# Four-stage transformer block: first tile's rows of the experts fetched in the second attention; its first batch loaded and normalised beside the end of the first attention

## The chip, the cores and the metric

The program runs on one core of a Trainium2 chip. The metric is the device time of one execution in microseconds; of several executions the median is taken. Engines are named as in the profile: PE is TensorE's matmul, PEld its weight load, DVE is VectorE, ACT is ScalarE, POOL is GpSimd, SP is SyncE, which here only issues DMAs.

## What is computed

Input x is 8 batches of 512 tokens of 256 numbers, in float32. Two layers follow each other:

```
xn = layernorm(x)
x  = x + attention0(xn) + ffn0(xn)
xn = layernorm(x)
x  = x + attention1(xn) + experts(xn)

attention0: latents of 128, 16 heads of 64, rotary positions, full softmax
ffn0:       256 -> 1024 -> 256 with binarised weights, gelu
attention1: 16 heads of 16, q = elu(q) + 1, k = elu(k) + 1, causal sums
            out = q . cumsum(k v) / max(q . cumsum(k), 1e-6)
experts:    gate = softmax(xn @ Wg + bg), the best 2 of 8 experts chosen
            for e in 8: out += chosen[e] * (relu(xn @ W1[e] + b1[e]) @ W2[e] + b2[e])
```

The result of a matmul must hold float32 accuracy: each factor is split into a high part and a rest ("hi" and "lo"), and three matmuls (L103 to L105) make one product.

## The kernel before

The program is four stages, one after the other: stage_f (ffn0 and the latents), stage_a (attention0), stage_b (attention1 and the choice of the experts), stage_c (the experts). Each stage is a block with a program for each engine; a block ends when every engine is through, and its last DMAs are among that. Only then does the next block begin. The order within an engine is written out by hand; engines wait for each other on semaphores.

**End of stage_a.** DVE inverts the last denominators (`invert`, L1065), ACT takes over the last values (L1147), PE projects, DVE adds (L1122), and SP stores the last batch in mid_x and waits for it.

**Stage_b** works batch by batch, in slots t = 0 to 3. Its head, L1390 to L1421 on SP, fetches batch 0 of x, the identity, the raw weights q, k and v, ten small tables (`later`), batch 1, and 2 MB of the first expert's weights. DVE then runs `norm_variance(0)`, `norm(0)`, the low halves of the weights (L1731), waits for all ten tables, makes batch 0 in four slots `make(0, t)`, and then does `norm_variance(1)`, `norm(1)`, before the loop over batches. `make(b, 3)` on DVE holds `weigh_experts` and `choose`. ACT runs `norm_root(0)`, the high halves of the weights (L1845), `make(0, t)`, `norm_root(1)`. PE transposes the normalised batch (L1448), projects (L103 to L105), and goes into the loop: scores (L1487), then the transposes of batch 1. POOL writes each token's row to the lists of its two experts by indirect DMA (L1924); ACT pads the end of every list with one tile of rows that point to a spare token (L1839).

**Stage_c** runs eight experts e. Expert e has as many tiles of 256 tokens as its list needs (`tiles_of`, a value loaded from `trips`). In this run they are 7, 5, 3, 7, 1, 1 for e = 0 to 5 and 12 for the last two together. SP loads a tile's rows (L2048) into the one buffer c_x_t, PE transposes them (L2068), ACT and DVE make hi and lo, PE makes eight `up` and eight `down` products (m = 0 to 7), ACT and DVE turn each `up` into h_hi and h_lo (L2128, L2154), DVE adds the bias to y (L2168), POOL adds y's rows to the output (L2198) by token numbers that it has fetched (`load_ids`, L2187). There is one buffer y: DVE may write it only when `y_free` is given, which POOL does in `settle` (L2206) once the rows of the tile before have landed. In the kernel before, `settle` stands at the head of POOL's loop over tiles, and a first one is let through by a counted semaphore.

The weights of expert e + 2 are split while expert e (1 to 5) runs: in tile i, ACT casts piece k = 0 to 3 at m = 0, 2, 4, 6 (`cast`, L2114) and DVE subtracts (`split_low`, L2147). Tile 0 does the first half of the weights, tile 1 the second, and so in turn. POOL does the last piece always, and all four of the second half where the expert has one tile (`late`, L2234), **after** the tiles of e and before the next `settle`. One piece is a cast (L2177) and a subtraction (L2182). For e = 0 POOL splits all of w1 before its loop, and w2 in chunks within the loop with at least one chunk after it (`rest`, L2227).

```
                    if by_engines(e):
                        pool.wait_ge(tile_splits, e)
                        with pool.Fori(pool.value_load(late[0:1, e:e + 1], ...
```

## Time and profile before

| what | value |
|---|---|
| runs | 2082.5, 2083.79, 2087.86 us; median 2083.79 |
| the profiled execution | 2079.97 us, of which the span is 2078.3 us |
| PE busy | 1882.9 us, 91% of the span |
| DVE, ACT, POOL busy | 60%, 45%, 61% |
| mean granted TensorE clock | 0.964 of full |
| stage_f and stage_a | up to 1243.56 us |
| stage_b | 1243.56 to about 1599.7 us |
| stage_c | 1599.7 us to the end |

The profile is one execution. PE's busy share is high in every stage, so what counts is where PE stands idle and what ends that idle time: a timeline row shows it in square brackets. The granted clock is 1.00 when TensorE runs at 2.4 GHz and 0.50 at 1.2 GHz.

### The profile page before, as it was taken

How to read it: one execution, taken by the hardware profiler on the slowest of the kernel's cores; microseconds unless marked ns; L12 is line 12 of the kernel's file. 1: busy time of each engine (PE TensorE's matmuls, PEld its weight loads, DVE VectorE, ACT ScalarE, POOL GpSimd, SP SyncE). 2: the span in 40 equal slices, each digit the busy share in tenths (PEclk: the TensorE clock that was granted, in tenths of full speed). 3: DMA queues.
4: the chain of work that ended last, by engine and by line, in shares of the span. 5: the costliest groups of instructions: out<-in, count | busy, mean ns of one | idle time of the engine just before them, and what ended most of it. 6: DMA issues, size and time to landing. Idle time of an engine off the chain costs nothing. (4 is left out here: it accounts for less than half of the span.)

```text
span 2078.3 us, 35394 instructions
## 1 busy us (share of the span) xinstructions
PE 1882.9 (91%) x12820; PEld 1311.8 (63%) x12820; DVE 1244.4 (60%) x1819; ACT 931.8 (45%) x1605; POOL 1270.1 (61%) x824
## 2 busy tenths in 40 slices
PE   6997799999999999999999976888883899998998
PEld 5887444544545454454544545676762899998998
DVE  5775466656565666656666525776763566656343
ACT  5885344334343433434334224433320456776554
POOL 3553588778687887868778643455463664435433
PEclk8999799999999999999999988999996899999999
DMA  4223322232231323213232202132224443332222
GB/s 138 102 107 113 107 58 64 50 96 62 72 82 31 92 62 84 62 38 92 52 102 52 62 32 105 41 96 68 72 67 148 133 86 81 85 77 53 37 47 42
DMA packets 82432, 158.35 MB, mean 76 GB/s; under 512 B 14680, under 2 KB 64088, under 8 KB 76496
## 3 DMA queue, kind: packets, MB, share of 16 engines
q1 hardware_dynamic: 64832, 130.50, 22.6%
q0 software_dynamic: 14592, 18.40, 5.6%
q10 hardware_dynamic: 2880, 7.73, 1.0%
q8 instruction: 82, 1.34, 0.3%
q14 instruction: 46, 0.38, 0.1%
HBM read 80.45 MB, written 44.15 MB: 60 GB/s over the span
## 5 line engine op out<-in xcount | busy, mean ns | idle before, releaser
L1162 ACT ACTIVATE a_pr<-a_pT 128x1024 f32<-128x1024 f32 x256 | 261.8, 1023 | 425.3 <-PE a_pT L940 425.3
L1195 POOL TENSOR_TENSOR a_total<-a_total,a_pr 128x1024 f32<-128x1024 f32 x128 | 320.6, 2505 | 148.9 <-ACT a_pr L1162 148.5
L1051 DVE TENSOR_REDUCE a_row_max<-a_pG 128x2 f32<-128x1024 f32 x256 | 309.1, 1220 | 144.6 <-PE a_pG L914 144.3
L953 PE MATMUL a_pA<-a_pr,a_v 128*64 128x512 f32 x1024 | 277.4, 620 | 0.1
L2154 DVE TENSOR_TENSOR c_h_lo<-c_h,c_h_hi 128x256 fp32r<-128x256 f32 x288 | 151.3, 532 | 181.3 <-ACT c_h_hi L2128 181.0
L2128 ACT ACTIVATE c_h<-c_pU,c_b_c 128x256 f32<-128x256 f32 x288 | 140.8, 489 | 177.9 <-PE c_pU L105 176.6
L1195 POOL TENSOR_TENSOR a_total<-a_pr 128x1024 f32<-128x1024 f32 x64 | 151.7, 2370 | 51.4 <-ACT a_pr L1162 51.1
L1176 POOL TENSOR_TENSOR a_by_cos<-a_by_cos,a_swapped 128x1024 f32<-128x1024 f32 x64 | 155.4, 2429 | 36.7 <-DMA a_swapped<-a_by_sin 36.6
L1183 POOL TENSOR_TENSOR a_qk_lo<-a_by_cos,a_qk_hi 128x1024 fp32r<-128x1024 f32 x64 | 158.7, 2480 | 2.3 <-ACT a_qk_hi L1130 2.3
L1045 DVE TENSOR_TENSOR a_by_sin<-a_pG,a_sin 128x1024 f32<-128x1024 f32 x64 | 78.3, 1224 | 129.4 <-PE a_pG L105 124.7
L2198 POOL DMA_INDIRECT out_x<-c_y,c_ids x72 | 118.0, 1639 | 40.8 <-DVE c_y L2168 24.1
L2128 ACT ACTIVATE c_h_hi<-c_pU,c_b_c 128x256 fp32r<-128x256 f32 x288 | 139.9, 486 | 0.0
L914 PEld LDWEIGHTS a_pG<-a_qk_hi 64*128 64x128 f32 x512 | 45.9, 186 | 143.7 <-issue 91.0
L914 PE MATMUL a_pG<-a_qk_hi 64*128 64x512 f32 x512 | 120.8, 489 | 5.1 <-ACT a_qk_hi L1130 3.8
L1130 ACT CAST a_qk_hi<-a_by_cos 128x1024 fp32r<-128x1024 f32 x64 | 67.0, 1046 | 110.3 <-POOL a_by_cos L1176 110.3
L103 PE MATMUL c_pU<-c_xT_hi,d_w_lo 128*128 128x256 f32 x368 | 108.8, 296 | 7.3 <-remote 6.2
L935 PE MATMUL a_pT<-a_qk_hi,a_qk_lo 64*128 64x512 f32 x512 | 113.2, 436 | 1.9 <-ACT a_pr L1162 1.7
L103 PE MATMUL c_pY<-d_w_hi,c_h_lo 128*128 128x256 f32 x368 | 105.5, 287 | 8.5 <-DVE c_h_lo L2154 8.3
L940 PE MATMUL a_pT<-a_neg_max,a_ones 64*128 64x512 f32 x512 | 108.9, 419 | 0.0
L104 PE MATMUL c_pU<-c_xT_lo,d_w_hi 128*128 128x256 f32 x368 | 106.7, 290 | 0.0
L105 PE MATMUL c_pU<-c_xT_hi,d_w_hi 128*128 128x256 f32 x368 | 105.9, 288 | 0.0
L953 PEld LDWEIGHTS a_pA<-a_pr,a_v 128*64 128x64 f32 x1024 | 50.8, 135 | 86.9 <-issue 85.9
(271 smaller groups left out, 4986.3 us busy)
## 6 DMA issues: line engine op xcount, KB each, us to landing
a_swapped<-a_by_sin SPq DMA_DIRECT2D x256, 128.0 KB, 2.3
a_inv_by_head<-mid_inverses SPq DMA_DIRECT2D x30, 512.0 KB, 5.8
c_x_t<-mid_rows SPq DMA_DIRECT2D x37, 272.0 KB, 2.9
mid_latents<-f_c_parts SPq DMA_DIRECT2D x8, 1024.0 KB, 3.9
a_latent_parts<-mid_latents SPq DMA_DIRECT2D x8, 1024.0 KB, 7.4
d_raw<-in_weights SPq DMA_DIRECT2D x3, 2048.0 KB, 8.2
c_raw<-in_weights SPq DMA_DIRECT2D x3, 2048.0 KB, 7.7
f_x_t<-in_x SPq DMA_DIRECT2D x8, 512.0 KB, 3.8
```

The lines of the kernel that those rows point to most:

```text
L103: nc.tensor.matmul(out, l_lo, r_hi, start=start, stop=False, **kw)
L914: last = nc.tensor.matmul(pair[:, h, :], qk_hi[rows, u % RQ, 0, t * P:(t + 1) * P], qk_hi[rows, u % RQ, 1, :], start=True, stop=True)
L935: nc.tensor.matmul(pT[:, h, :], k[rows, 1, ks], q[rows, 0, :], start=(i == 0), stop=False)
L953: last = nc.tensor.matmul(pA[64 * h:64 * h + 64, :], v[:, t, p, h, :], pr[:, n % RP, h, :], start=(t == 0), stop=(t == NT - 1))
L1051: nc.vector.reduce_max(row_max[:, u % 2, :, t], pair[:], AX.X).then_inc(read, 1)
L1162: nc.scalar.activation(pr[:, n % RP, :, :], pT[:], ACT.Exp, scale=SCALE).then_inc(exp_done, 1)
L1176: nc.gpsimd.tensor_tensor(by_cos[:, u % 2, :, :], by_cos[:, u % 2, :, :], swapped[:], ALU.add).then_inc(rope_done, 1)
L1183: nc.gpsimd.tensor_tensor(qk_lo[:, u % RQ, :, :], by_cos[:, u % 2, :, :], qk_hi[:, u % RQ, :, :], ALU.subtract).then_inc(qk_lo_done, 1)
L1195: nc.gpsimd.tensor_tensor(total[:, u % 2, :, :], before, pr[:, n % RP, :, :], ALU.add).then_inc(summed, 1)
L2128: nc.scalar.activation(dst[:, m % RH, :], pU[m % RH][:], ACT.Relu, bias=b1_c[:, e, m:m + 1]).then_inc(relu_done[m % RH], 1)
L2154: nc.vector.tensor_tensor(h_lo[:, m % RH, :], h[:, m % RH, :], h_hi[:, m % RH, :], ALU.subtract).then_inc(h_lo_done[m % RH], 1)
L2198: pool.indirect_dma_start(out=out, out_offset=bass.IndirectOffsetOnAxis(ap=ids[:, t:t + 1], axis=0), in_=y[:, t, :], in_offset=None, compu ...
```

## The change

Names with `ahead` are tensors that now live over stages a, b and c: the identity, batch 0 of x, its normalised form xm (whose first half later takes the first expert tile), and raw q. The change does the following.

- In stage_a, SP loads batch 0 of x and raw q in the middle of the stage; DVE takes the variances before its last `invert`, ACT the root after its last copy, DVE normalises after `invert`.
- In stage_b the head is shorter: SP begins with raw k and v, then batch 1, then the tables. DVE goes `make(0, 0)`, `norm_variance(1)`, `make(0, 1)`, `norm(1)`, `make(0, 2)`, the wait for the tables, `weigh_experts(0)`; `choose(0)` comes after the first mask in the loop.
- At the end of stage_b, SP fetches the rows of the first expert's first tile; the first list gets two tiles of padding, and its number of tiles is at least two.
- Stage_c begins with the transposes of that tile. ACT, not SP, loads b1 and the weights of expert 3; SP begins with the second tile.
- POOL's `settle` stands at the end of each tile, and the first `y_free` comes from DVE.
- POOL's late pieces for expert e + 2 come **before** the tiles of e. ACT's cast of piece k = 3 waits for them.

```diff
@@ stage_a, SP
                     if u == 2 * NP:
                         sp.dma_start(tokens(x1, B), tokens(x1, 0)).then_inc(spare_done, 16)
+                        for dst, src in ((ahead.x, tokens(x1, 0)), (ahead.raw_q, l1_wq)):
+                            sp.dma_start(dst[:], src).then_inc(ahead_in, 16)
@@ stage_a, DVE
+                ahead_variance()
                 for half in range(2):
                     invert(UNITS // GROUP - 1, half)
+                ahead_norm()
@@ stage_a, ACT
                 take_values(UNITS - 1)
+                act.wait_ge(ahead_step, 2 * NT + 1)
+                nc.scalar.activation(small[:, 1, :], small[:, 0, :], ACT.Sqrt).then_inc(ahead_root, 1)
@@ stage_b, SP
-                load(0)
-                sp.dma_start(ident[:], ident_d).then_inc(ident_in, 16)
-                for i, (n, (src, _)) in enumerate(names.items()):
-                    sp.dma_start(raw[n][:], src).then_inc(raw_in[i], 16)
+                for n in "kv":
+                    sp.dma_start(raw[n][:], names[n][0]).then_inc(raw_in[n], 16)
+                load(1)
...
                         if b == B:
                             store(b - 2)
+                            first_rows()
@@ stage_b, DVE
-                dve.wait_ge(loaded, 16 * LATER)
-                for t in range(NT):
-                    make(0, t)
-                norm_variance(1)
-                norm(1)
+                make(0, 0)
+                norm_variance(1)
+                make(0, 1)
+                norm(1)
+                make(0, 2)
+                dve.wait_ge(loaded, 16 * LATER)
+                weigh_experts(0)
...
+                        if b == 0 and t == 0:
+                            choose(0)
@@ stage_c, ACT
+                    if k == PIECES // 2 - 1:
+                        act.wait_ge(late_done, e - 2)
                     nc.scalar.copy(w_hi[w][:, at], raw[w][:, at]).then_inc(cast_done[k], 1)
...
-                x_high()
+                act.dma_start(b1_c[:], b1).then_inc(b1_in, 16)
+                x_high(False)
                 load_weights(nc.scalar, 1)
                 act.dma_start(b2_row[:], b2).then_inc(b2_in, 16)
                 load_weights(nc.scalar, 2)
+                load_weights(nc.scalar, 3)
@@ stage_c, DVE
                 x_low()
+                dve.sem_inc(y_free, 1)
@@ stage_c, POOL
                 for e in range(NE):
+                    if by_engines(e):
+                        wait_raw(pool, e + 2)
+                        with pool.Fori(pool.value_load(late[0:1, e:e + 1], ...), PIECES // 2) as i:
+                            split_high(e + 2, i * PIECE + WIDE // 2, PIECE)
+                            split_low(e + 2, i * PIECE + WIDE // 2, PIECE)
+                        pool.sem_inc(late_done, 1)
                     with pool.Fori(0, tiles_of(pool, e)) as i:
-                        settle()
                         load_ids(row_of(e, i))
...
                         send()
...
+                        settle()
-                    if by_engines(e):
-                        pool.wait_ge(tile_splits, e)
...
-                        pool.sem_inc(splits, 1)
-                settle()
```

In `cast(e + 2, ...)` the number waited for is `(e + 2) - 2`, so in expert e ACT waits until POOL has done the pieces of this same e. The wait stands in every tile of the expert; from the second tile on it is met already.

The first place where order matters is DVE at the head of stage_b, before:

```order
L1731 TENSOR_TENSOR b_wv_lo<-b_raw_v,b_wv_hi 128x528
L1617 TENSOR_TENSOR b_xT_lo<-b_pG,b_xT_hi 128x512 x2
L1624 SCALAR_TENSOR_TENSOR b_qT<-b_pG,b_ex 128x512 x2
L1624 SCALAR_TENSOR_TENSOR b_kT<-b_pG,b_ex 128x512 x2
L1677 TENSOR_TENSOR b_lg<-b_lg,b_bg_row 128x32
...
L1702 TENSOR_SCALAR b_sel<-b_rank 128x32
L1592 BN_STATS b_stats<-b_x_t 128x6 x4
...
L1611 TENSOR_SCALAR b_xm<-b_x_t,b_small 128x256 x4
L1632 TENSOR_TENSOR d_scores<-b_pA,b_causal 128x2048
```

and now:

```order
L1773 TENSOR_TENSOR b_wv_lo<-b_raw_v,b_wv_hi 128x528
L1659 TENSOR_TENSOR b_xT_lo<-b_pG,b_xT_hi 128x512 x2
L1634 BN_STATS b_stats<-b_x_t 128x6 x4
...
L1666 SCALAR_TENSOR_TENSOR b_qT<-b_pG,b_ex 128x512 x2
L1647 RECIPROCAL b_small<-b_small 128x4
...
L1653 TENSOR_SCALAR b_xm<-b_x_t,b_small 128x256 x4
L1666 SCALAR_TENSOR_TENSOR b_kT<-b_pG,b_ex 128x512 x2
L1719 TENSOR_TENSOR b_lg<-b_lg,b_bg_row 128x32
...
L1674 TENSOR_TENSOR d_scores<-b_pA,b_causal 128x2048
L1688 TENSOR_TENSOR b_state<-b_pS,b_blocks 128x512
...
L1744 TENSOR_SCALAR b_sel<-b_rank 128x32
```

The statistics and xm of batch 1 have moved from behind the choice (b_sel) to between the features q and k of batch 0, and the choice itself behind the first mask and state.

The second place is POOL in stage_c between two experts. The rows between the sends of one expert's last tile and the next expert's first sends, before (c_ids_f is the fetch of the token numbers, `f_ones_set` the old name of the semaphore number that `settle` waits on, y_sent):

```order
L2198 DMA out_x<-c_y,c_ids 4352x256
L2234 TENSOR_LOAD d_late [waits f_base_done]
...
L2177 COPY d_w_hi<-d_raw 128x512
...
L2182 TENSOR_TENSOR d_w_lo<-d_raw,d_w_hi 128x512
...
L2014 TENSOR_LOAD d_trips
...
L2206 ISA [waits f_ones_set]
...
L2187 DMA c_ids_f<-mid_rows 128x2x1
L2193 CAST c_ids<-c_ids_f 128x2 [waits f_sign2_done,f_b2_in]
```

and now (there `settle` waits on the number once called f_w2s_in):

```order
L2256 DMA out_x<-c_y,c_ids 4352x256
L2264 ISA [waits f_w2s_in]
...
L2277 TENSOR_LOAD d_late [waits f_y_done]
...
L2235 COPY c_w_hi<-c_raw 128x512
...
L2240 TENSOR_TENSOR c_w_lo<-c_raw,c_w_hi 128x512
...
L2066 TENSOR_LOAD d_trips
...
L2245 DMA c_ids_f<-mid_rows 128x2x1
L2251 CAST c_ids<-c_ids_f 128x2 [waits f_ones_set,f_ln_in]
```

The settle has moved ahead of the pieces, and the pieces now belong to the expert whose tiles follow.

The third place is ACT in the first tile of an expert, at m = 5 to 7, now:

```order
L2185 ACTIVATE c_h<-c_pU,c_b_c 128x256
L2185 ACTIVATE c_h_hi<-c_pU,c_b_c 128x256
L2169 ISA [waits f_g_lo_done]
L2169 COPY d_w_hi<-d_raw 128x512
L2076 ISA [waits f_c_bias_done]
L2185 ACTIVATE c_h<-c_pU,c_b_c 128x256
L2185 ACTIVATE c_h_hi<-c_pU,c_b_c 128x256
L2160 CAST c_xT_hi<-c_pX 128x256 [waits f_diag_done] x2
```

The row with f_g_lo_done is the new wait (late_done has that number); before, this cast had none. Behind it on ACT stand the two activations of m = 7 and the casts of the next tile's rows.

## Rows read from the trace of the kernel before

**Rows 1.** Timeline, end of stage_a, DVE (start us, length us, instruction, [idle before <-releaser])

```profile
1222.34 3.37 DVE L1065 RECIPROCAL a_inv<-a_pD 128x256 f32<-128x256 f32 x2 [10.87 <-PE a_pD L962]
...
1230.39 1.45 DVE L1119 TENSOR_TENSOR a_att<-a_att,a_pT 128x512 f32<-128x512 f32 x2 [4.68 <-PE a_pT L997]
```

**Rows 2.** Timeline, head of stage_b up to the first projection

```profile
1247.44 1.41 DVE L1592 BATCH_NORM_STATS2 b_stats<-b_x_t 128x6 f32<-128x256 f32 x4 [7.24 <-DMA b_x_t<-mid_x]
...
1250.65 0.63 ACT L1845 CAST b_wv_hi<-b_raw_v 128x528 fp32r<-128x528 f32 x1
...
1251.69 1.94 PE L1448 MATMUL b_pG<-d_ident,b_xm 128*128 128x128 f32 x8 [11.96 <-DVE b_xm L1611]
...
1255.22 0.77 PE L103 MATMUL b_pG<-b_xT_hi,b_wq_lo 128*128 128x512 f32 x1 [1.58 <-DVE b_xT_lo L1617]
```

**Rows 3.** Timeline, stage_b, from batch 0's choice to batch 1's first projection

```profile
1271.78 0.22 DVE L1692 TENSOR_TENSOR b_more<-b_gate 128x64 f32<-128x64 f32 x1
...
1274.99 1.41 DVE L1592 BATCH_NORM_STATS2 b_stats<-b_x_t 128x6 f32<-128x256 f32 x4
...
1279.23 1.94 PE L1448 MATMUL b_pG<-d_ident,b_xm 128*128 128x128 f32 x8 [6.71 <-DVE b_xm L1611]
...
1286.58 0.58 PE L103 MATMUL b_pG<-b_xT_hi,b_wq_lo 128*128 128x512 f32 x1
```

**Rows 4.** Timeline, stage_c's start up to the first product

```profile
1608.92 1.11 PE L2068 MATMUL c_pX<-d_ident,c_x_t 128*128 128x128 f32 x4 [13.19 <-DMA c_x_t<-mid_rows]
...
1611.16 0.58 PE L103 MATMUL c_pU<-c_xT_hi,d_w_lo 128*128 128x256 f32 x1 [1.13 <-DVE c_xT_lo L2141]
```

**Rows 5.** Timeline, stage_c, first expert: POOL and DVE at the first tile

```profile
1618.01 1.04 POOL L2177 CAST c_w_hi<-c_raw 128x1024 fp32r<-128x1024 f32 x1 [41.33 <-DMA c_raw<-in_weights]
...
1634.42 0.76 DVE L2168 TENSOR_TENSOR c_y<-c_pY,c_b_row 128x256 f32<-128x256 f32 x2 [4.45 <-POOLq L2206]
...
1635.05 0.79 POOL L2187 DMA_DIRECT2D c_ids_f<-mid_rows  x1 [2.26 <-remote]
```

**Rows 6.** Timeline, last tile of expert 0 and first two of expert 1

```profile
1708.13 0.88 DVE L2168 TENSOR_TENSOR c_y<-c_pY,c_b_row 128x256 f32<-128x256 f32 x2 [0.34 <-PE c_pY L105]
...
1712.11 4.04 DVE L2147 TENSOR_TENSOR d_w_lo<-d_raw,d_w_hi  x1
...
1712.63 2.96 POOL L2182 TENSOR_TENSOR c_w_lo<-c_raw,c_w_hi  x1
...
1718.56 2.61 POOL L2182 TENSOR_TENSOR c_w_lo<-c_raw,c_w_hi  x1 [0.24 <-POOL c_w_hi L2177]
...
1724.81 0.76 DVE L2168 TENSOR_TENSOR c_y<-c_pY,c_b_row 128x256 f32<-128x256 f32 x2 [0.31 <-remote]
...
1736.65 0.76 DVE L2168 TENSOR_TENSOR c_y<-c_pY,c_b_row 128x256 f32<-128x256 f32 x2 [0.31 <-remote]
...
1745.23 0.78 POOL L2187 DMA_DIRECT2D c_ids_f<-mid_rows  x1 [3.29 <-DMA out_x<-c_y,c_ids]
```

**Rows 7.** Busy time by stretch: stretch, length, PE, PEld, DVE, ACT, POOL, clock, DMA, GB/s

```profile
1710.00:1720.00 10.00, 7.77 (x58) 7.57 (x57) 8.66 (x9) 6.00 (x17) 8.04 (x5) 0.89 0.25 28
1720.00:1730.00 10.00, 10.00 (x82) 10.00 (x82) 6.75 (x14) 6.91 (x19) 5.19 (x5) 0.94 0.23 41
```

**Rows 8.** Timeline, last tile of expert 3, experts 4 and 5, second tile of expert 6

```profile
1890.81 0.76 DVE L2168 TENSOR_TENSOR c_y<-c_pY,c_b_row 128x256 f32<-128x256 f32 x2 [0.31 <-remote]
...
1899.23 0.62 ACT L2114 CAST d_w_hi<-d_raw  x1
...
1915.84 1.26 POOL L2182 TENSOR_TENSOR d_w_lo<-d_raw,d_w_hi  x1 [0.24 <-POOL d_w_hi L2177]
1917.59 0.61 POOL L2177 CAST d_w_hi<-d_raw  x1 [0.49 <-POOL d_w_lo L2182]
...
1921.20 0.75 DVE L2168 TENSOR_TENSOR c_y<-c_pY,c_b_row 128x256 f32<-128x256 f32 x2 [6.15 <-POOLq L2206]
...
1951.98 0.88 DVE L2168 TENSOR_TENSOR c_y<-c_pY,c_b_row 128x256 f32<-128x256 f32 x2 [0.34 <-PE c_pY L105]
```

More of the change, by code:

```diff
@@ L667, with stage_a @@
 GROUP = 4
-def stage_a(nc, spent, wq_t, wk_t, wv_t, wo_t, rope_c, rope_s, neg_blocks_d, ident_d, one_row_d, part, latents, inverses, x1):
+def stage_a(nc, spent, wq_t, wk_t, wv_t, wo_t, rope_c, rope_s, neg_blocks_d, ident_d, one_row_d, part, latents, inverses, x1, l1_wq, ahead):
     with ExitStack() as ctx:
@@ L679, in stage_a @@
         sb, sem = st.sb, st.lasting
-        ident = sb("ident", [P, P])
+        ident = ahead.ident
+        stats = sb("stats", [P, NT, 6])
+        mean_var = sb("mean_var", [P, NT, 2])
+        small = sb("small", [P, 4, NT])
         neg_blocks = sb("neg_blocks", [P, NT, P])
@@ L1225, in stage_b @@
 def stage_b(nc, wq_t, wk_t, wvg_t, wo_t, bg, own2_d, causal_d, blocks_d, before_d, ident_d,
-            lower_d, ids_d, starts_d, thresholds_d, weights, x1, out, dens, invs, rows, dispatch):
+            lower_d, ids_d, starts_d, thresholds_d, weights, x1, out, dens, invs, rows, ahead, dispatch):
     with ExitStack() as ctx:
@@ L1239, in stage_b @@
         sb, sem = st.sb, st.lasting
-        ident = dispatch.ident
+        ident = ahead.ident
         own2 = sb("own2", [P, 2])
@@ L1249, in stage_b @@
         w_lo = {n: sb(f"w{n}_lo", [P, f], F32R) for n, (_, f) in names.items()}
-        raw = {n: sb(f"raw_{n}", [P, f]) for n, (_, f) in names.items()}
+        raw = {"q": ahead.raw_q, "k": sb("raw_k", [P, KC * D]), "v": sb("raw_v", [P, KC * VG])}
         RX = 4
-        x_t = sb("x_t", [P, RX, NT, D])
+        x_t = [ahead.x] + [sb(f"x_t{i}", [P, NT, D]) for i in range(1, RX)]
         RM = 3
-        xm = sb("xm", [P, RM, NT, DW])
+        xm = [ahead.xm] + [sb(f"xm{i}", [P, NT, DW]) for i in range(1, RM)]
         stats = sb("stats", [P, NT, 6])
@@ L1303, in stage_b @@
         loaded = sem("loaded")
-        ident_in = sem("ident_in")
-        raw_in = [sem(f"raw_in{i}") for i in range(3)]
+        raw_in = {n: sem(f"raw_in_{n}") for n in "kv"}
         w_split = sem("w_split")
@@ L1838, in end_experts @@
                         count = act.value_load(counts[0:1, e:e + 1], min_val=0, max_val=T)
[L1839 to L1842 removed]
+                        for at in range(e * CAP, e * CAP + (TILE if e else 2 * TILE), TILE):
+                            act.dma_start(rows[bass.ds(count + at, TILE), :].rearrange("(t p) d -> p t d", p=P),
+                                          pad[:]).then_inc(padded, 16)
+                act.sem_inc(root, 1)
                 for i, n in enumerate(names):
[L1844 removed]
+                    if n != "q":
+                        act.wait_ge(raw_in[n], 16)
                     nc.scalar.copy(w_hi[n][:], raw[n][:]).then_inc(w_split, 1)
+                make(0, 0)
+                norm_root(1)
+                make(0, 1)
+                make(0, 2)
                 act.wait_ge(fills, 2)
[L1847 to L1849 removed]
+                make(0, 3)
                 for b in range(B):
@@ L1954, in _, with stage_c @@
                     pool.wait_ge(sent[i], 32 * NT * ((B - 1 - i) // RM + 1))
-def stage_c(nc, weights, b1, b2, rows, out, dispatch):
+def stage_c(nc, weights, b1, b2, rows, out, ahead, dispatch):
     with ExitStack() as ctx:
@@ L1966, in stage_c @@
         sb, sem = st.sb, st.lasting
-        ident, trips, rest, late = dispatch.ident, dispatch.trips, dispatch.rest, dispatch.late
+        ident, trips, rest, late = ahead.ident, dispatch.trips, dispatch.rest, dispatch.late
         RW = 3
@@ L2086, in down @@
                             last.then_inc(down_done, 1)
-                transposes()
+                transposes(ahead.xm[:, 0:TB, :])
                 for e in range(NE):
@@ L2264, in one_rows, with tile_ends @@
             m[DH * h + g, g, DH * h:DH * h + DH] = 1.0
+    return m
+def tile_ends():
+    m = np.tile(TILE * np.arange(1, MAX_TRIPS, dtype=np.float32), (P, NE, 1))
+    m[:, 0, 0] = -1.0
     return m
@@ L2352, in program @@
     spent = stage_f(nc, *of("x w1_rows w1_t w2_t b1 b2 wd_t ln_sb ident_d part latents"))
-    stage_a(nc, spent, *of("wq_t wk_t wv_t wo_t rope_c rope_s neg_blocks ident_d one_row part latents inverses x1"))
     with ExitStack() as ctx:
+        ahead = Ahead(nc, ctx)
+        stage_a(nc, spent, *of("wq_t wk_t wv_t wo_t rope_c rope_s neg_blocks ident_d one_row part latents inverses x1 "
+                               "l1_wq"), ahead)
         dispatch = Dispatch(nc, ctx)
         stage_b(nc, *of("l1_wq l1_wk l1_wvg l1_wo bg own2_d causal_d blocks_d before_d ident_d lower_d ids starts "
-                        "thresholds weights x1 out dens invs rows"), dispatch)
-        stage_c(nc, *of("weights e_b1 e_b2 rows out"), dispatch)
+                        "thresholds weights x1 out dens invs rows"), ahead, dispatch)
+        stage_c(nc, *of("weights e_b1 e_b2 rows out"), ahead, dispatch)
 def kernel(**inputs):
```

113 lines of the change are left out of this document (70 added, 43 removed).

## The prediction

> **What bounds the kernel now.** I read the page first: PE is busy for 1882.9 of 2078.3 us, so a step is worth what it takes out of PE's idle time, or puts in. Then the timeline of PE and of what released it, at four places. At the end of stage_a DVE has gaps, because it waits for PE [rows 1]. At the head of stage_b PE stands for 11.96 us until batch 0 is loaded and normalised [rows 2]. Between batches 0 and 1 it stands for 6.71 us, since DVE normalises batch 1 only behind the choice of experts [rows 3]. At the head of stage_c it stands for 13.19 us for one tile's rows [rows 4], and DVE's first y then waits 4.45 us for POOL [rows 5]. After that I read y: DVE writes one per tile, from 1724.81 to 1736.65 in expert 1, so a free tile takes 11.84 us. A tile that takes longer shows a wait. The change of expert shows what POOL and ACT do there [rows 6 to 8].
>
> **What it gains.** All is set against the profiled execution of 2079.97 us; the median is 3.8 above it.
>
> *Stage_a, 0.* The variances of batch 0 cost about what those of batch 1 do: statistics 1.41 and some 0.6 of small operations [rows 2]. They lie in DVE's 10.87 idle before `invert`; xm, 1.4 plus 0.5 for the root's results, lies in the 4.68 before the next row [rows 1]. If that cover failed, it would cost at most these 3.9 us.
>
> *Head of stage_b, −5.1.* The transposes can begin at about 1243.7, 8.0 earlier than at 1251.69. But on ACT the casts of the transposed x stand behind the cast of raw v. Raw k and v now lead the queue, with about the bytes of batch 0, which came in at 1247.44, 3.9 after the stage began. So: 1247.4, the cast of v (0.63), one more cast of x (0.6), and then the 1.58 which the projection waited behind its transposes before: 1250.2 in place of 1255.22, which I round to 5.1. Bounds: 8.0 if nothing waits; 3.9 if the weights land 1.2 later.
>
> *Batch 1 earlier, −7.3.* Statistics and xm of batch 1 now stand ahead of the features of batch 0, where DVE waited for PE anyway. The 6.71 of idle goes, and with it some 0.6 that the transposes had to wait for x's casts. The first projection of batch 1 comes at 1279.3 on the old clock, for 1286.58. The choice, 1271.78 to 1274.99, 3.2 us [rows 3], now stands behind the first mask. Bounds: 3.2 if DVE becomes what ends it, and 8.5. The first_rows fetch at the end of stage_b is issued over 10 us before the last store, which hides it.
>
> *Head of stage_c, −9.2.* The transposes wait for no load. `up` begins 2.24 after them [rows 4], so at 1602.0 for 1611.16, and w1 lands as much earlier, for it too is no longer behind other loads.
>
> *First y, −2.3 more.* What holds the second y is POOL: the split of w1 (from 1618.01), then 2.26 for the first `settle`, then the numbers at 1635.05, and `y_free` only after that tile's sends [rows 5]. The first settle's idle falls away, since DVE gives the first `y_free`. 9.2 + 2.3 = 11.5. Bounds: 9.2 (PE is what holds the second y), and 13.7 with all 4.45 of DVE's wait.
>
> Sum of the gains: 5.1 + 7.3 + 11.5 = 23.9.
>
> **What it loses.** This is POOL's late piece, now ahead of the tiles, and ACT's wait for it in tile 0, with two activations and the next x casts behind it. Let Y be the time of the y of the last expert's last tile. POOL must send Y's rows, and settle them. The fetch of numbers behind a settle came 8.6 after y (1736.65 to 1745.23) [rows 6]. Then comes a load of the count, 0.6, and one piece: cast 0.61, gap 0.24, subtraction 1.26, together 2.1, with 0.4 for the signal: Y + 11.7. ACT reached its k = 3 cast at 8.4 after y (1890.81 to 1899.23) [rows 8]. So ACT stands 3.3 us. Some 0.9 of it is slack, for PE runs ahead by one product; PE stands 2.4. The cost of a stop is more: where PE was busy 7.77 us of 10, the granted clock was 0.89, and 0.94 in the next 10 us, in which PE was never idle [rows 7]. At half clock that is (1.1 + 0.6), 1.7 us of work.
>
> - *Experts 2 and 3:* 2.4 + 1.7 = 4.1 each, **+8.2**.
> - *Expert 1:* here settle comes first, then a chunk of `rest`, some 4.2 with its 2.61 subtraction [rows 6], then the piece: 8.6 + 0.7 + 4.2 + 0.6 + 3.0 + 0.4 = 17.5. The y comes 3.6 behind it, at 21.1; before it came 16.7 after (1708.13 to 1724.81). 4.4, and 2.1 for the clock: **+6.5**.
> - *Experts 4 and 5*, one tile each: four pieces, 2.6 apart (subtraction at 1915.84, next cast at 1917.59 and so next subtraction 0.85 later) [rows 8]: 8.6 + 0.6 + 10.0 + 0.4 = 19.6; y of 4 comes 3.6 later at 23.2. The same again: y of 5 at 46.4. Two free tiles, 23.7, bring the second y of expert 6 to 70.1, and the half clock after two long stops some 2.2: 72.3. Before, it came at 61.2 (1890.81 to 1951.98), and that held its own waits, 6.15 among them (1921.20). **+11.1**.
>
> Sum of the losses: 8.2 + 6.5 + 11.1 = 25.8. Net +1.9 us: the likeliest is **no change**, 2083.8 + 1.9, about **2086**.
>
> A rule on contention. DVE's subtraction of 1712.11 began first, lasted 4.04 us, and ended (1716.15) only after POOL's, which ran from 1712.63 for 2.96. So the two slowed each other, and the earlier was slowed too [rows 6]. The Trainium skill (SBUF — State Buffer, "Who interferes with whom") says that a DVE instruction with two SBUF inputs contends with a GpSimd instruction that reads SBUF, and that whoever issues first holds the shared ports for the whole instruction while the other fully blocks. By that rule a late piece would be held for at most one subtraction of DVE; the row here does not agree that the first goes unharmed. By the row I take the cast and subtraction free where ACT and so DVE stand, and leave up to 1 us a piece for the range: 5 first pieces, +5 at most.
>
> **The rivals.**
> - *A, faster: the wait on POOL is nearly free.* If ACT's cast comes late of itself (the two casts and DVE's part of the weights are slowed by the earlier k = 0 to 2) or POOL's settle by 2 to 3 us sooner than 8.6, only experts 4 and 5 lose. For it: 3.3 us is a small number, made as a difference of two measured ones. Against it: for experts 4 and 5 it is 11 us. It gives 2083.8 − 23.9 + 11.1 = 2071; with half of that too, 2065. The least of all is 2060, if nothing is lost.
> - *B, slower: POOL's chain is longer than I take it.* Place: between settle and late_done of experts 1 to 5. Point: from 1 us more a piece on. A contended piece costs up to 3.0 (the rest's subtraction took 2.61 to 2.96 for twice the width [rows 6]), and every microsecond goes into PE's stand in full, five times for the first pieces and six more for the others. +5 to +11: 2091 to 2097.
> - *C, slower: the head of stage_b gives little.* If k and v land late, or DVE, with batch 1's work put ahead of the features, holds batch 0's scores, 5.1 + 7.3 shrinks to 3.9 + 3.2: +5.3, 2091.
> - *D: the change does not do what it says.* If the padding of two tiles or the wait for tables on DVE undid the early start, PE would stand at stage_c's head as before: +11.5, 2097. Nothing in the order speaks for it. I give it little.
>
> **How the numbers follow.** Under about 0.3% (6.2 us) a difference can't be told from none with this kernel. My forecast of 2086, with 2080 to 2092 as its own range for the slack and the clock, takes 0.46. A takes 0.24, B 0.18, C 0.07, D 0.05. Faster by over that bound is A and 0.04 from the forecast's lower end: 0.28. Slower is 0.16 of B, 0.04 of C, D, and 0.05 from the forecast's upper end: 0.30. The same is the rest, 0.42. The range runs from 2065, which is A with half of the loss of experts 4 and 5, to 2097, the end of B and D; outside lie the best part of A and mishaps added up.
>
> **What would show it.** In the profile of the changed kernel: DVE's variances in stage_a with no new idle on PE; transposes at the very start of stage_b, and the first projection 6.6 after it; no 6.7 us stop ahead of batch 1's transposes; stage_c about 12.4 earlier, and `up` 2.3 after its start. Then ACT idle ahead of the weights' cast, released by POOL's late subtraction: about 3.3 for experts 2 and 3, 5 for expert 1, 9 to 11 for 4 and 5, with PE's clock below 1 behind each. I am wrong if those waits are absent or twice as long, if y spacing at a change of expert is not some 14 us (2 and 3), 21 (1) and 23 (4 and 5), or if stage_b ends at the same distance from its start.

## The result and the profile after

| | kernel before | changed kernel |
|---|---|---|
| median, 12 runs each | 2085.43 us (2082.50 to 2087.86) | 2090.67 us (2086.52 to 2096.07) |
| ratio | | 1.0029, 95% interval 1.0022 to 1.0037 |
| span of the profiled execution | 2078.3 us | 2090.7 us |

On another occasion the changed kernel took 2085.97 us, the kernel before 2084.26, with a ratio of 1.0007 (0.9997 to 1.0018). So the change costs something between nothing and 6 us, at the edge of what can be measured. Some 24 us of standing were removed, and some 28 were added.

Timeline of PE in the changed kernel, with the two ACT rows that the first projection waits behind, at the places of [rows 2 to 4]: stage_b's first transposes, batch 0's and batch 1's first projections, stage_c's first transposes and first product.

```profile
1247.78 1.97 PE L1491 MATMUL b_pG<-ahead_ident,ahead_xm 128*128 128x128 f32 x8 [3.92 <-DVEq L1770]
...
1251.37 0.63 ACT L1893 CAST b_wv_hi<-b_raw_v 128x528 fp32r<-128x528 f32 x1 [0.40 <-DMA b_raw_v<-in_l_wvg]
...
1251.91 1.07 ACT L1820 CAST b_xT_hi<-b_pG 128x512 fp32r<-128x512 f32 x2
...
1254.09 0.76 PE L103 MATMUL b_pG<-b_xT_hi,b_wq_lo 128*128 128x512 f32 x1 [4.34 <-DVE b_xT_lo L1659]
...
1278.11 0.47 PE L103 MATMUL b_pG<-b_xT_hi,b_wq_lo 128*128 128x512 f32 x1 [0.88 <-DVE b_xT_lo L1659]
...
1597.12 0.63 PE L2118 MATMUL c_pX<-ahead_ident,ahead_xm 128*128 128x128 f32 x4 [3.91 <-PEq L1420]
...
1598.94 0.57 PE L103 MATMUL c_pU<-c_xT_hi,d_w_lo 128*128 128x256 f32 x1 [1.19 <-DVE c_xT_lo L2198]
```

PE's idle time ahead of stage_b is 3.92 us instead of 11.96, and ahead of stage_c 3.91 instead of 13.19. What is left passes while one block ends and the next begins: no load is named any more, only the sequencers of DVE and PE. The stop of 6.71 us before batch 1 is gone. So all three heads work as the diff says. Yet the first product of stage_c is only 12.2 us earlier on the clock (1611.16 to 1598.94), because stage_b began 4.1 us later than before (1.8 us of that is there at stage_a's first store already, ahead of anything that the change adds but tensors' places), and this execution then lost about 4 more within stage_b, of which more below.

Timeline of POOL, ACT and DVE in the changed kernel, at the change to expert 1 (the last y of expert 0 is at 1695.49) and to expert 2 (the last y of expert 1 is at 1766.06):

```profile
1704.70 1.32 POOL L2235 CAST c_w_hi<-c_raw  x1 [1.75 <-issue]
1706.27 2.89 POOL L2240 TENSOR_TENSOR c_w_lo<-c_raw,c_w_hi  x1 [0.24 <-POOL c_w_hi L2235]
...
1710.31 0.61 POOL L2235 CAST d_w_hi<-d_raw  x1 [1.15 <-issue]
1711.15 1.26 POOL L2240 TENSOR_TENSOR d_w_lo<-d_raw,d_w_hi  x1 [0.24 <-POOL d_w_hi L2235]
1712.80 0.62 ACT L2169 CAST d_w_hi<-d_raw  x1 [4.22 <-POOLq L2280]
...
1716.29 0.79 DVE L2226 TENSOR_TENSOR c_y<-c_pY,c_b_row 128x256 f32<-128x256 f32 x2 [0.31 <-DMA f_b_rows<-in_b]
```

```profile
1769.54 1.56 POOL L2256 DMA_INDIRECT out_x<-c_y,c_ids  x1 [0.30 <-issue]
...
1774.59 0.61 POOL L2235 CAST c_w_hi<-c_raw  x1 [3.49 <-issue]
1775.45 1.28 POOL L2240 TENSOR_TENSOR c_w_lo<-c_raw,c_w_hi  x1 [0.25 <-POOL c_w_hi L2235]
...
1777.12 0.62 ACT L2169 CAST c_w_hi<-c_raw  x1 [2.59 <-POOLq L2280]
...
1780.62 0.76 DVE L2226 TENSOR_TENSOR c_y<-c_pY,c_b_row 128x256 f32<-128x256 f32 x2 [0.32 <-DMA f_b_rows<-in_b]
```

Each chain reads the same way. POOL sends the rows of the last y, waits for their landing, does a piece (behind the chunk of `rest`, for expert 1), and signals (L2280); ACT's k = 3 cast comes right behind it. It stood 4.22 us for expert 1, 2.59 for expert 2, 5.08 for expert 3, and, with four pieces, 10.74 for expert 4 and 9.45 for expert 5. The row of POOL's sequencer names no DMA for the idle time ahead of a piece (`issue`); that it is the landing follows from the program, where `settle` stands there. The same for PE, clock included (columns as in [rows 7]):

```profile
1700.00:1710.00 10.00, 7.70 (x53) 7.49 (x52) 7.64 (x8) 3.75 (x10) 7.17 (x4) 0.83 0.15 19
1710.00:1720.00 10.00, 6.29 (x34) 6.09 (x33) 2.91 (x7) 3.98 (x10) 4.66 (x6) 0.70 0.12 28
1720.00:1730.00 10.00, 10.00 (x83) 10.00 (x83) 5.76 (x13) 7.03 (x18) 2.13 (x2) 0.95 0.33 48
```

In [rows 7], the same place in the kernel before, PE was busy 7.77 us of 10 and the clock was 0.89. Here there are two stops, PE is busy 6.29 of 10 in the second, and the clock falls to 0.70.

### The profile page after: what moved, and what is told of

The parts are those of the page before. It is cut to its first block and busy times, and to the rows that moved or that the text cites. A ratio compares the mean times of both kernels' runs of the same rounds, so it can differ in the third digit from the quotient of the medians.

```text
span 2090.7 us, 35360 instructions
## 1 busy us (share of the span) xinstructions
PE 1893.6 (91%) x12820; PEld 1319.0 (63%) x12820; DVE 1227.4 (59%) x1819; ACT 931.3 (45%) x1603; POOL 1267.2 (61%) x826
## 3 DMA queue, kind: packets, MB, share of 16 engines
q8 instruction: 82, 1.34, 0.3%
## 5 line engine op out<-in xcount | busy, mean ns | idle before, releaser
L2212 DVE TENSOR_TENSOR c_h_lo<-c_h,c_h_hi 128x256 fp32r<-128x256 f32 x288 | 146.7, 513 | 230.6 <-ACT c_h_hi L2185 223.5
L1219 POOL TENSOR_TENSOR a_qk_lo<-a_by_cos,a_qk_hi 128x1024 fp32r<-128x1024 f32 x64 | 156.8, 2450 | 2.3 <-ACT a_qk_hi L1164 2.3
```

The lines of the kernel that those rows point to most:

```text
L1219: nc.gpsimd.tensor_tensor(qk_lo[:, u % RQ, :, :], by_cos[:, u % 2, :, :], qk_hi[:, u % RQ, :, :], ALU.subtract).then_inc(qk_lo_done, 1)
L2212: nc.vector.tensor_tensor(h_lo[:, m % RH, :], h[:, m % RH, :], h_hi[:, m % RH, :], ALU.subtract).then_inc(h_lo_done[m % RH], 1)
```

## The experiments

Four quantities are read from each profile. **A** is the time between the stores of batches 0 and 2 in stage_a, thus of two batches; the expectations below call the second store that of batch 1, with the same numbers. **V** is one step of stage_a within A: from the transposition of the maxima (L931) of head pair 18 to that of pair 19, the first step whose data is swapped behind the two loads. **U** is the start of stage_c's first product. **C** is the time from the last y of expert 0 to the last y of all, and three stretches of it: the first two y of expert 1, the y from the first of expert 2 to the second of expert 3, and from the y of expert 4 to the second of expert 6 (each counted from the y ahead of it). The last column holds the median and the ratio to the kernel before on the same occasion. There were four occasions: before and changed; late_after to c_loads_itself; middle_loads_alone to rest_behind; and change_again, pool_order_alone and heads_only (4 to 12 runs each). The kernel before took 2085.43, 2084.94, 2084.17 and 2084.26 us on them.

| kernel | A | V | U | C | exp. 1 | exp. 2, 3 | exp. 4 to 6 | median, ratio (interval) |
|---|---|---|---|---|---|---|---|---|
| before | 250.4 | 12.8 | 1611.2 | 362.3 | 28.5 | 59.6 | 61.2 | |
| changed | 253.7 | 14.9 | 1598.9 | 387.3 | 35.1 | 68.3 | 70.8 | 2090.67, 1.0029 (1.0022 to 1.0037) |
| change_again | 254.2 | 16.6 | 1593.3 | 387.5 | 35.1 | 68.4 | 70.9 | 2085.97, 1.0007 (0.9997 to 1.0018) |
| late_after | 253.9 | 17.0 | 1591.0 | 374.1 | 27.9 | 62.5 | 71.5 | 2074.38, 0.9945 (0.9927 to 0.9964) |
| settle_behind | 254.1 | 16.6 | 1591.8 | 371.7 | 33.3 | 60.4 | 64.8 | 2070.13, 0.9938 (0.9916 to 0.9960) |
| choice_back | 253.4 | 14.9 | 1597.5 | 387.2 | 35.1 | 68.6 | 70.3 | 2094.26, 1.0044 (1.0031 to 1.0056) |
| c_loads_itself | 256.6 | 17.4 | 1609.2 | 387.3 | 35.2 | 68.3 | 70.7 | 2092.16, 1.0032 (1.0017 to 1.0048) |
| middle_loads_alone | 251.7 | 14.9 | 1621.5 | 362.7 | 28.5 | 59.6 | 61.6 | 2087.72, 1.0012 (1.0002 to 1.0023) |
| loads_at_end | 250.0 | 12.8 | 1589.1 | 387.3 | 35.1 | 68.4 | 70.7 | 2087.81, 1.0019 (1.0010 to 1.0028) |
| both_mended | 251.5 | 12.8 | 1590.2 | 371.5 | 33.4 | 60.1 | 64.9 | 2071.02, 0.9939 (0.9925 to 0.9952) |
| rest_behind | 249.9 | 12.8 | 1594.4 | 371.3 | 29.8 | 63.4 | 65.0 | 2071.46, 0.9935 (0.9915 to 0.9954) |
| pool_order_alone | 249.8 | 12.8 | 1617.5 | 387.9 | 34.0 | 69.2 | 71.6 | 2106.84, 1.0106 (1.0089 to 1.0123) |
| heads_only | 250.1 | 12.8 | 1590.0 | 362.9 | 28.5 | 59.7 | 61.6 | 2060.45, 0.9891 (0.9875 to 0.9908) |

**late_after.** The pieces behind the tiles again, without ACT's wait.

```diff
                 for e in range(NE):
-                    if by_engines(e):
-                        wait_raw(pool, e + 2)
-                        with pool.Fori(pool.value_load(late[0:1, e:e + 1], ...), PIECES // 2) as i:
...
                     with pool.Fori(0, tiles_of(pool, e)) as i:
...
+                    if by_engines(e):
+                        pool.wait_ge(tile_splits, e)
+                        with pool.Fori(pool.value_load(late[0:1, e:e + 1], ...), PIECES // 2) as i:
...
@@ cast
-                    if k == PIECES // 2 - 1:
-                        act.wait_ge(late_done, e - 2)
```

> The change, but POOL's late pieces stand behind the tiles of their expert again, as in the kernel before, and ACT's k = 3 cast waits for nothing. Everything else of the change stays. Theory (the late pieces ahead of the tiles cost what the heads gain): the y of expert 1 comes 16.7 us after the one before it, those of experts 2 and 3 some 12, expert 5 to 6 as before, and the whole is 23 to 26 us faster than the changed kernel, about 2066. Rival (the loss lies in stage_b, whose batches took 38.0 us instead of 37.4, and in stage_a): at most 15 us faster, 2076 or more.

Measured: 16.3 us faster than the changed kernel's first median, 11.6 faster than its second: between theory and rival, or within the rival. Expert 1 lost its wait (27.9), experts 2 and 3 most of theirs (62.5 for 59.6 before). Experts 4 to 6 did not: 71.5 us, 10 more than in the kernel before, though the pieces stand where they stood there. What differs from it is `settle`. The next row of POOL behind the sends of expert 4's y shows it:

```profile
1892.32 1.56 POOL L2254 DMA_INDIRECT out_x<-c_y,c_ids  x1 [0.30 <-issue]
1897.71 0.61 POOL L2233 CAST d_w_hi<-d_raw  x1 [3.83 <-issue]
```

POOL now waits 3.83 us for the landing and only then starts the four pieces, and the numbers of the next tile are fetched behind them. In the kernel before, the landing passed beside the pieces. The delays add up: for expert 4's y (1883.73) the numbers were fetched 3.3 us after it (1887.07), in the kernel before 2.1 us ahead of it (1900.84 for 1902.91). So the place of `settle` has a price of its own. heads_only, below, has the pieces behind the tiles too but `settle` at their head, and its C is 362.9: 11.2 us less.

**settle_behind.** The change, but `settle` at the head of each tile, with a first count on y_sent in place of DVE's first y_free.

```diff
+                        settle()
                         load_ids(row_of(e, i))
...
-                        settle()
```

> The change, but settle stands at the head of each tile again (with a first count for it), so that POOL does the late pieces between the last send and the wait for its landing, not behind it. Theory (it is the landing of the last rows, some 4 us, that makes late_done too late): late_done comes near 8 us after y instead of near 12, so ACT's stand at experts 2 and 3 nearly goes (y spacing 12 to 13 us for 14.6 and 17.2), and experts 4 and 5 gain 2 to 4 us each; first y 2 us later. Together 8 to 12 us faster than the changed kernel, about 2080. Rival (the number of pieces is what counts, or contention with DVE): within 3 us of the changed kernel.

The timeline of POOL and ACT at expert 2 (the y ahead of it is at 1757.44):

```profile
1760.92 1.57 POOL L2255 DMA_INDIRECT out_x<-c_y,c_ids  x1 [0.30 <-issue]
...
1761.90 1.22 POOL L2234 CAST c_w_hi<-c_raw  x1
...
1763.36 1.52 POOL L2239 TENSOR_TENSOR c_w_lo<-c_raw,c_w_hi  x1 [0.25 <-POOL c_w_hi L2234]
...
1766.55 0.62 ACT L2169 CAST c_w_hi<-c_raw  x1
...
1766.93 0.78 POOL L2244 DMA_DIRECT2D c_ids_f<-mid_rows  x1 [2.05 <-DMA out_x<-c_y,c_ids]
```

The piece is done 7.4 us after y (1764.88) instead of 10.7 (1776.73 in the changed kernel), ACT's cast waits for nothing, and the stop is gone: 60.4 us for 68.3. C is 15.7 us shorter. The median is 20.5 us below the changed kernel's first and 15.8 below its second; what the first has beyond C lies ahead of stage_c, where profiles of one program differ by as much. The mechanism was the theory's, its size larger than the 8 to 12 expected: experts 4 to 6 gained 6.0 us and experts 2 and 3 7.9, about as the theory has them, but expert 1 gained 1.8 that were not in its sum, and the 2 us to be lost at the first y came out as 0.3 (from U to the last y of expert 0, 96.88 for 96.55).

**choice_back.** Batch 0's `choose` before the loop and `norm_variance(1)`, `norm(1)` behind it, on ACT `norm_root(1)` last.

> The change, but in stage_b DVE makes the choice of batch 0 before the loop, and normalises batch 1 behind it, as before; ACT's root likewise. Theory (this part gains 7.3 us at batch 1 and nothing of it is lost later): 7 us slower than the changed kernel, 2098, with 38.0 us from batch to batch unchanged. Rival (the new phase of DVE against PE and ACT, set by this order, makes each later batch 0.6 us longer): the batches take 37.4 us again, so the loss is only 3 to 4 us.

Measured: 3.6 us slower than the changed kernel's first median, with intervals that overlap, and 8.3 slower than its second. In the trace batch 1's first projection comes 30.9 us after batch 0's, for 24.0 in the changed kernel: 6.9 us, as the theory says. Three batches on, the distance from batch 0 is 98.9 us for 93.9, so 5.0 are left. Behind that its batches take 37.9 us on average (most of them 37.4), the changed kernel's 38.6. Those are the rival's numbers, and so is a loss of 3.6. But late_after, settle_behind and c_loads_itself, which have the change's own order, show 37.4 too on the same occasion, so the order does not make the difference (see change_again). The gain at batch 1 is shown; its whole size in the median is not.

**c_loads_itself.** Stage_c fetches its first tile; b1 and the weights of expert 3 still come from ACT.

```diff
-                            first_rows()
@@ stage_c
-                    with sp.Fori(0 if e else 1, tiles_of(sp, e)) as i:
+                    with sp.Fori(0, tiles_of(sp, e)) as i:
-                transposes(ahead.xm[:, 0:TB, :])
+                seen(pe, x_in, 16)
+                transposes(x_t)
...
-                x_high(False)
+                x_high()
```

(Line numbers of this kernel are some 617 higher in stages b and c: its file holds stage_b's beginning twice, and the second is what runs.)

> The change, but stage_c loads its first tile itself, as before; stage_b's end has no fetch of rows. Theory (the fetch saves 9 us of standing at the head of stage_c): 8 to 10 us slower than the changed kernel, 2099 to 2101, and stage_b's batches unchanged. Rival (the fetch at the end of stage_b delays its last stores, and gives part of it back): 5 to 7 us slower, with the end of stage_b earlier relative to its last projection.

```profile
1603.92 4.82 SPq L2717 DMA_DIRECT2D c_x_t<-mid_rows  x2
...
1606.92 1.11 PE L2734 MATMUL c_pX<-ahead_ident,c_x_t 128*128 128x128 f32 x4 [8.63 <-DMA c_x_t<-mid_rows]
```

The stand is 8.63 us here, 13.19 before [rows 4], 3.91 with the change. So of the 9.3 us only 4.7 are the early fetch; the other 4.6 come from the order of the loads. Here the tile lands 3.0 us after its issue, ahead of all weights. In the kernel before it was issued behind b1 and 2 MB of weights, at 1602.18, and PE began 6.7 us after that (1608.92); the weights themselves landed at 1608.06. The other 0.8 us went by ahead of the issue. The Trainium skill (DMA: Bandwidth & Descriptors, "Issuing engines are not separate DMA queues") says that loads started by different engines run on the same 16 DMA engines, and that starting them elsewhere saves only the time to start them. The rows agree: ACT starts its weights only behind the first transposes (1608.18), so nothing large is on its way beside the tile. That it is this order and not the issuing engine that helped is concluded and not shown, for no run has this order with SP issuing all. In time the early fetch is not shown: the median moved by 1.5 us only, neither theory's number (the batches of the profile were the longest of all).

**change_again.** The changed kernel a second time.

> The changed kernel once more, for a second profile of it. Theory (the 38.0 us from batch to batch in stage_b of its first profile belong to that execution and not to the program, since three kernels with the same stage_b showed 37.4): 37.4 us between most batches, the stretch between the stores of batches 0 and 1 of stage_a over 253 us, and the y times of stage_c spaced as in the first profile within 0.5 us. Rival (38.0 belongs to this program): 38.0 again.

A, C and the three stretches of C are the same within 0.6 us. V is not (14.9 and 16.6, see loads_at_end), and stage_b is not: four batches (3 to 7) took 154.6 us in the first profile and 152.5 now, and most of them 38.0 again, so my theory as put is wrong. But 38.0 is not of the program either: two kernels with the old stage_b (middle_loads_alone and pool_order_alone) show 38.0, and late_after, settle_behind and c_loads_itself, with the new one, 37.4. Over nine profiles with the new order these four batches took 150.5 to 157.9, mean 153.1; over three with the old, 150.5 to 156.8, mean 153.3. The profile that the prediction rests on was one of the shortest.

**middle_loads_alone.** The kernel before, and two loads more.

```diff
                         sp.dma_start(tokens(x1, B), tokens(x1, 0)).then_inc(spare_done, 16)
+                        for dst, src in ((extra_x, tokens(x1, 0)), (extra_q, l1_wq)):
+                            sp.dma_start(dst[:], src).then_inc(ahead_in, 16)
```

> The kernel before, with nothing but the two loads of the change in the middle of stage_a added (batch 0 of x, 512 KB, and raw q, 256 KB), into tensors that nobody reads. Theory (those two loads, in a stretch where the queues already carry the copy of batch 0, delay loads that PE waits for): the stretch between the stores of batches 0 and 1 of stage_a takes 253.5 us or more for 250.35, and the whole is 3 us slower, 2088. Rival (the longer stretch seen in five profiles comes from the tensors' new places or from chance): 250 to 251 us there, and no difference in the whole.

Measured: ratio 1.0012 (1.0002 to 1.0023), about 2.5 us slower, with A only 1.4 longer in its profile (251.7): less than the theory's 253.5, more than the rival's 251. V is clearer: 14.90 us for 12.77, and PE stands there at the same point and for as long as in the changed kernel (below):

```profile
506.64 0.50 PE L920 MATMUL a_pG<-a_qk_hi 64*128 64x512 f32 x2 [1.44 <-ACT a_qk_hi L1136]
```

**loads_at_end.** The change, with the two loads behind SP's loop in stage_a.

> The change, but the loads of batch 0 of x and of raw q stand behind SP's loop in stage_a, where the DMA queues carry nothing (the last 40 us). Theory: the stretch between the stores of batches 0 and 1 is 250.4 us again, the end of stage_a stays where it is relative to the store before it (the loads land over 10 us before DVE wants them), and the whole is 3 to 4 us faster than the changed kernel, 2087. Rival (DVE then waits for the load and the last invert is late): no faster, and stage_a's last stretch over 52 us.

**both_mended** adds the settle of settle_behind to it.

> The change with settle at the head of the tiles and with the two loads at the end of stage_a. Theory (the two act in different stages and add up): 3 to 4 us faster than with settle moved alone, 2067. Rival (the slack is taken up elsewhere): 2070 as with settle alone.

A is 250.0 and 251.5. All six profiles of kernels with the whole change and the loads in the middle show 253.4 to 256.6; the six without any load there, or with it at the end, 249.8 to 251.5. V separates them better: 12.76 to 12.79 us in those six, 14.90 to 17.38 in all seven with the loads in the middle, middle_loads_alone among them. The end of stage_a is unharmed: from store 6 to store 7 it takes 53.4 and 52.2 us, in the three kernels without the early normalisation 52.7 to 53.1.

This is the step in the kernel before:

```profile
499.05 2.37 POOL L1176 TENSOR_TENSOR a_by_cos<-a_by_cos,a_swapped 128x1024 f32<-128x1024 f32 x1 [0.83 <-DMA a_swapped<-a_by_sin]
...
499.85 0.33 PE L921 MATMUL a_pG<-a_ident,a_row_max 128*128 128x128 f32 x1
...
512.62 0.30 PE L921 MATMUL a_pG<-a_ident,a_row_max 128*128 128x128 f32 x1 [0.38 <-DVE a_row_max L1051]
```

and in the changed one:

```profile
492.84 2.50 SPq L840 DMA_DIRECT2D a_swapped<-a_by_sin  x4
...
500.68 0.33 PE L931 MATMUL a_pG<-ahead_ident,a_row_max 128*128 128x128 f32 x1
...
502.62 2.48 POOL L1212 TENSOR_TENSOR a_by_cos<-a_by_cos,a_swapped 128x1024 f32<-128x1024 f32 x1 [3.58 <-DMA a_swapped<-a_by_sin]
...
506.33 0.51 PE L924 MATMUL a_pG<-a_qk_hi 64*128 64x512 f32 x2 [1.44 <-ACT a_qk_hi L1164]
...
515.58 0.30 PE L931 MATMUL a_pG<-ahead_ident,a_row_max 128*128 128x128 f32 x1 [0.37 <-DVE a_row_max L1061]
```

Of every head pair, SP swaps rows of q and k for the rotation (`a_swapped`, four small DMAs of which POOL's addition waits). The two new loads are issued at 491.56 and 492.23, right ahead of these four, which land at 502.56 instead of 498.98, though the stage is only 0.8 us later here (500.68 for 499.85). POOL waits for them 3.58 us instead of 0.83, ACT's cast (505.14) and PE's scores follow in a chain, and PE stands 1.44 us. PE's busy time, clock, DMA share and GB/s in the 20 us around it, of the kernel before, the changed one and change_again:

```profile
500.00:520.00 20.00, 19.62 (x106) 1.00 0.12 27
```

```profile
500.00:520.00 20.00, 17.86 (x92) 1.00 0.17 38
```

```profile
500.00:520.00 20.00, 17.82 (x85) 0.91 0.12 27
```

So the loads cost 2.1 us by V where the clock stayed at 1.00 (changed, choice_back, middle_loads_alone), and 3.8 to 4.6 in the four profiles where it also fell to a mean of 0.90 over the step, behind a stop that was as long in two of them (1.44 and 1.48 us). At the end of the stage the loads cost nothing that these numbers show. The rest of A's 3.3 us in the first pair of profiles can't be put down to them: a later step, in which PE waits for the next latents, took 13.7 us in the profile of the kernel before and 14.8 or more in every other one, loads or none (16.1 in the changed kernel, with a clock of 0.89).

In the medians none of this is shown. loads_at_end is 2.9 us faster than the changed kernel's first median and 1.8 slower than its second (ratios 1.0019 for 1.0029 and 1.0007), and both_mended gives 2071.02 where settle_behind gave 2070.13, which is the rival's number and not the 2067 expected.

**rest_behind.** Both_mended, and for expert 1 the late piece ahead of the last chunk of w2.

> The last one, and in POOL's program before expert 1 the last chunk of w2 (rest) stands behind the late piece instead of ahead of it. Theory (ACT's wait in expert 1 is longer than in 2 and 3 because that chunk is ahead of the piece): the first y of expert 1 comes 16 to 17 us after the one before it for 20.2, and the whole is 3 to 5 us faster, 2063. Rival (DVE or PE is what then holds expert 1, as in the kernel before, where the y came 16.7 us after without any wait of ACT): 3.5 us in the trace there, and with the chunk still split while expert 1 runs, nothing more.

The first y of expert 1 comes 18.2 us after the one before it, for 20.2, and the second after 11.6, for 13.2: 3.6 us gained there. Expert 3 lost 3.3 in the same profile, where ACT waited 2.37 us for a piece that started late, and the median did not move (2071.46). A gain in one place with no gain in the whole, which is the rival's reading; why expert 3 lost I leave open.

**pool_order_alone.** The kernel before, with the change's whole order on POOL, ACT's wait, and y_free from DVE.

> The kernel before with nothing but the change's order on POOL: late pieces ahead of the tiles, settle at the end of each tile, the first y_free from DVE, and ACT's wait. Theory: from the last y of expert 0 to the last y of all 387.3 us instead of 362.3, less some 2 us gained at the first y: 22 to 23 us slower than the kernel before, 2107. Rival (the loss of 25 us comes only in company with the earlier head, through the order of the weights' loads or other tiles' phases): less than 15 us slower.

Measured: 22.6 us slower, ratio 1.0106 (1.0089 to 1.0123). C is 387.9 us. The cost belongs to POOL's order alone and needs none of the heads.

**heads_only.** Both_mended with the pieces behind the tiles.

> The change without its new order on POOL: settle at the head of the tiles, the late pieces behind the tiles of their expert, no wait on ACT, and the two loads at the end of stage_a. Theory (the heads gain some 21 us in all, up to the first product of stage_c, and POOL's new order gave 25 of them back, 9 with settle alone moved): the y times of the experts are spaced as in the kernel before, and the whole is 20 us faster than it, 2064. Rival (an earlier start of stage_c meets other waits, as w6's landing at expert 5, which give it back): 2070 or more, no better than with settle alone moved.

Measured: **2060.45 us, ratio 0.9891 (0.9875 to 0.9908)**, 24 us faster than the kernel before and the fastest of all. C is 362.9 us, that of the kernel before (362.3). The gain of the heads is real and survives to the end.

With this run C stands for all four orders of POOL (the place of the two loads does not touch it, 387.3 either way): 387.3 with the pieces ahead of the tiles and `settle` behind, 374.1 with both behind, 371.5 to 371.7 with both ahead, 362.9 with the pieces behind and `settle` ahead, as in the kernel before. Moving `settle` costs 15.7 or 11.2 us, moving the pieces (with ACT's wait) 13.2 or 8.7, and both together 24.4.

## Why the prediction was right, and where it was not

The forecast was no change, 2086, as a small difference of two sums of about 24 and 26. Both sums are borne out, and 2090.67 lies in the own range given for that case. The mechanism of the losses, POOL's chain and ACT's wait for it, is the one that the runs show. That the net is so close is in part luck: two terms failed, some 3.4 us in stage_a and 1.9 at the first y, and the three other gains came out 2.2 us larger than forecast. By its steps:

- *Stage_a, 0: wrong.* The DVE and ACT additions are hidden, as forecast. But the step counted the instructions that work on the data, and not the two loads that bring it. They stand ahead of the small DMAs for the next head pair's rotation, and by V cost 2.1 to 4.6 us, 3.4 on average over the six profiles of the change (12.8 to 16.2). Without it the profiles' net, below, would be about 1 us; with it, it is 4 to 5.
- *Head of stage_b, 5.1: right.* From the last store of stage_a to the first projection: 14.99 before, 9.74 with the change, and 9.42 to 9.61 in nine more profiles: 5.3 to 5.6. The wait is as described: PE's transposes were done at 1249.75, but ACT's casts of the transposed x (1251.91) came right behind the cast of v (1251.37), which had waited for v's landing, and the row at 1254.09 waits 4.34 us for x's low half.
- *Batch 1 earlier, 7.3: right.* 31.36 us between the first projections before, 24.02 after: 7.34. Undone alone, 6.9 come back.
- *Head of stage_c, 9.2: right in size, half right in cause.* 9.3 by PE's idle time, but half of it, 4.6, by taking b1 and weights out of the tile's way (c_loads_itself).
- *First y, 2.3: wrong.* From U to the last y of expert 0 took 96.97 us before and 96.55 after, 0.4 less; and settle_behind, with the first `settle` restored, took 96.88, heads_only 96.50. The wait fell away at the first y and came back at the second and third (spacing 15.22 and 13.68 for 12.51 and 12.68), for POOL is what paces them. And POOL gained next to nothing: of its 2.26 us idle ahead of the first fetch of numbers, which the forecast put down to `settle`, 1.81 remained with no `settle` there:

```profile
1622.53 0.79 POOL L2245 DMA_DIRECT2D c_ids_f<-mid_rows  x1 [1.81 <-issue]
```

- *Losses, 25.8: right.* Measured in C: 25.0. Expert 1: 6.6 for 6.5. Experts 2 and 3 together: 8.7 for 8.2, but unevenly, 2.5 and 6.4 less 0.3 between them, for 4.1 each. At expert 3 the numbers for the last y of expert 2 (1804.06) were fetched only at 1804.13, where for the y ahead of expert 2 (1766.06) they were at 1763.09, and POOL's piece began 11.2 us after y instead of 8.5. The kernel before was as late there (fetch 1807.81, y 1807.84), and the forecast took the 8.6 of expert 1 for both. Experts 4 to 6: 9.6 for 11.1. ACT's k = 3 cast came 17.3, 11.1 and 19.4 us after y in experts 1, 2 and 4, for 17.5, 11.7 and 19.6, and 13.7 in expert 3; it stood 2.59 us for the 3.3 forecast in expert 2, and 5.08 in expert 3:

```profile
1817.71 0.62 ACT L2169 CAST c_w_hi<-c_raw  x1 [5.08 <-POOLq L2280]
...
1912.81 0.62 ACT L2169 CAST d_w_hi<-d_raw  x1 [10.74 <-POOLq L2280]
```

- *The halved clock, 1.7 a stop: right for experts 1 and 3* (second y 2.5 and 1.3 us late), *absent for expert 2*, whose granted clock stayed at 1.00 with PE busy 7.94 us of 10:

```profile
1775.00:1785.00 10.00, 7.94 (x67) 7.73 (x67) 4.81 (x11) 5.89 (x16) 2.31 (x4) 1.00 0.65 238
...
1810.00:1820.00 10.00, 5.45 (x46) 5.24 (x45) 2.76 (x8) 3.72 (x10) 4.26 (x4) 0.99 0.30 40
1820.00:1830.00 10.00, 10.00 (x73) 10.00 (x73) 5.74 (x13) 6.20 (x16) 3.54 (x4) 0.83 0.29 41
```

Rival A fell: no wait was met for free. Rival B's mechanism (a longer chain) did not occur: pieces behind a standing DVE took 0.60 to 0.64 (once 0.97, at expert 5) and 1.26 to 1.28. In settle_behind, beside a working DVE, the first pieces of experts 2 to 4 took 1.22 to 1.34 and 1.52 to 1.80, some 0.6 to 0.7 and 0.2 to 0.5 more. DVE's subtractions beside them take 0.42 and 0.68 where nothing contends. The Trainium skill's rule that the prediction cites (SBUF — State Buffer, "Who interferes with whom") allows for delays of that size, and these rows do not tell its blocking from sharing. What I had not put as a rival is that the place of `settle` alone can set whether the chain is late: with the pieces ahead of the tiles it is 15.7 of the 25 us.

Put together, as means over all profiles with either order: 5.7 us gained up to the first projection, 7.9 from there to batch 3's, 10.2 from batch 7's to stage_c's first product, and 0.4 at the first y, together 24.2; against them 3.4 in stage_a by V, or 4.0 by A, and 25.0 in stage_c. That is a net loss of 4 to 5 us; the medians of the two occasions gave 5.2 and 1.7. The side of the kernel before rests on three profiles for the first three figures.

## What to carry to other kernels

A wait for data to land, put ahead of work that does not need it, moves that work by the whole landing (here some 3.5 us each time): place the wait directly ahead of what it protects. When the step that you move ahead has loads of its own, count them in the stretch where they run, not where their data is used, and with them the small transfers that come right behind them in the program. A change with several independent parts can come out at nothing while one of its parts is worth over 1%; measure the parts alone before you drop or keep the whole.

## What the runs showed that I had not expected

Stage_b does not take the same time in every execution of the same instructions. In some profiles ACT's copies of the attention's output (slot 1 of a batch) start 0.2 us after PE's last matmul, in others 1.6, with 1.3 us of idle time whose releaser the profile can't name, in nearly every batch; the batch then takes 38.0 us for 37.4. Both patterns occur with both programs. They went with the occasion: all four profiles of the second occasion show 37.4, all seven of the third and fourth, on two other chips, 38.0; on the first the kernel before shows 37.4 and the changed one 38.0. I did not find the cause, and one profile against one profile would have read it as an effect of the change. From the first projection to U, the eight profiles with the change's own stage_b spread over 336 to 345 us.
